# Expert routing in a macaron transformer layer: table products in two halves, expert numbers compared by pairs, ranks summed by halves

## The reference

```python
scores = softmax(xf @ gate_w.T)
_, idx = top_k(scores + gate_b, K)                 # 6 experts for each token
weights = take_along_axis(scores, idx, axis=1)
order = argsort(idx.reshape(-1))                   # by expert, then by token
pos = arange(T * K) - starts[se]                   # rank of a token in its expert
xb = zeros((E, CAP, D)).at[se, pos].set(xf[tok], mode='drop')
h = silu(einsum(xb, w1)) * einsum(xb, w3); yb = einsum(h, w2)
y = scatter-add of yb * weights, for pos < CAP
z = silu(xf @ ws1.T) * (xf @ ws3.T) @ ws2.T        # the shared expert
return y + z
```

## Time and profile before

| | us |
|---|---|
| three runs | 1953.21, 1954.05, 1954.29 |
| median | 1954.05 |
| profiled execution, its device time | 1956.1 |
| profiled execution, first to last instruction (span) | 1954.0 |
| granted TensorE clock, mean share of full speed | 0.974 |

### The profile page before, as it was taken

One profiled execution on the slowest core, in us unless ns is written; L12 is line 12 of the kernel. 1 busy time (PEld: TensorE's weight loads), 2 busy tenths in 40 slices (PEclk: granted clock), 3 DMA queues, 4 the chain that ended last, 5 costly groups with the idle time before them and its releaser, 6 DMA issues. The chain is left out here.

```text
span 1954.0 us, 31890 instructions
## 1 busy us (share of the span) xinstructions
PE 1788.5 (92%) x10553; PEld 1098.4 (56%) x10554; DVE 1337.6 (68%) x3338; ACT 1095.2 (56%) x2260; POOL 836.5 (43%) x923
## 2 busy tenths in 40 slices
PE   6999998999955789999999999999799999989998
PEld 3666665777732344444455454445455656567776
DVE  4878787566537567777777777778268787866664
ACT  4767675111114567777777777776566767631111
POOL 1111110677646565555555555551000101027777
PEclk9999999999978899999999999999999999999999
DMA  2324341899943233333333333332213243339997
GB/s 81 120 86 135 96 125 63 247 258 252 246 74 86 78 85 104 99 95 105 100 98 99 104 102 95 107 91 68 66 49 106 93 139 93 106 97 265 262 265 157
DMA packets 192653, 244.05 MB, mean 125 GB/s; under 512 B 17578, under 2 KB 159978, under 8 KB 192494
## 3 DMA queue, kind: packets, MB, share of 16 engines
q1 hardware_dynamic: 166654, 202.97, 34.6%
q0 software_dynamic: 24576, 37.77, 10.1%
q10 hardware_dynamic: 1264, 1.31, 0.2%
HBM read 126.63 MB, written 63.86 MB: 97 GB/s over the span
## 5 line engine op out<-in xcount | busy, mean ns | idle before, releaser
L1352 DVE TENSOR_REDUCE a_smax<-a_p_ring 128x1 f32<-128x512 f32 (+2 forms) x768 | 353.7, 505 | 151.7 <-PE a_p_ring L1439 146.9
L1257 ACT ACTIVATE a_probs<-a_p_ring 128x512 f32<-128x512 f32 x640 | 364.1, 607 | 103.3 <-PE a_p_ring L1451 102.1
L1439 PE MATMUL a_p_ring<-p_ks,p_qs 100*128 100x512 bf16 (+3 forms) x1024 | 244.9, 304 | 43.2 <-ACT a_probs L1257 20.0
L48 POOL TENSOR_TENSOR f_rstd<-f_mv,eps 128x4 f32<-128x4 f32 x32 | 26.2, 818 | 539.0 <-DVE f_mv L42 534.5
L1451 PE MATMUL a_p_ring<-p_qs,p_ks 103*128 103x512 bf16 (+3 forms) x1024 | 243.7, 305 | 6.0 <-ACT a_probs L1257 5.3
L648 ACT ACTIVATE e_silu<-e_p_up 128x176 f32<-128x176 f32 x128 | 40.6, 317 | 352.8 <-PE e_p_up L738 352.8
L487 PE MATMUL f_p_up<-f_xnT,ws1T 128*128 128x512 f32 x384 | 186.8, 609 | 1.1 <-ACT f_xnT L280 1.1
L528 PE MATMUL f_p_z<-ws2T,f_hidden 128*128 128x256 f32 (+1 forms) x768 | 183.9, 390 | 1.9 <-DVE f_hidden L374 1.9
L127 POOL DMA_INDIRECT h_got<-rows,slot_token x128 | 126.0, 984 | 135.1 <-DVE slot_token L464 86.1
L1467 PE MATMUL a_p_out<-a_probs,p_v 128*32 128x512 f32 (+3 forms) x2048 | 176.6, 445 | 6.5 <-ACT a_probs L1257 6.5
L487 PE MATMUL f_p_up<-f_xnT,ws3T 128*128 128x512 f32 x384 | 180.6, 593 | 0.0
(11 more groups left out here) (156 smaller groups left out, 3573.7 us busy)
## 6 DMA issues: line engine op xcount, KB each, us to landing
h_w<-w_in SPq DMA_DIRECT2D x128, 352.0 KB
p_qs<-a_parts SPq DMA_DIRECT2D x192, 128.0 KB, 2.4
p_ks<-a_parts SPq DMA_DIRECT2D x192, 128.0 KB, 2.5
h_w<-w_in SPq DMA_DIRECT2D x128, 176.0 KB
rows<-f_row SPq DMA_DIRECT2D x32, 640.0 KB, 6.4
x<-x_in SPq DMA_DIRECT2D x16, 512.0 KB, 5.9
acc<-x SPq DMA_DIRECT2D x16, 512.0 KB, 3.3
a_x<-acc SPq DMA_DIRECT2D x16, 512.0 KB, 4.0
```

What stands on the lines that cost most here:

```text
L1257: nc.scalar.activation(to[:], p_score[s][:], ACT.Exp, scale=SCALE).then_inc(score_free[s], 1)
L1352: ins = nc.vector.tensor_reduce(smax[:, t, 4 * g + h:4 * g + h + 1], p_score[s][:, at:at + length], AX.X, ALU.max)
L1439: ins = nc.tensor.matmul(p_score[s][:, at:at + length], qs[1 - u][0:SR + MASK, 4 * g + h, t * P:(t + 1) * P], ks[1 - u][0:SR + MASK, 4 * g ...
```

## The change

Four edits, all in route_and_share.

1. The 24 table products of `add_to_table` are cut into two groups of 12. In a chunk with both neighbours the order on TensorE was turn, 24 products, turn; it is now 12 products, turn, 12 products, turn. The first 12 (tiles 0 and 1) wait for the first at_slot instruction only, the others for the second. In the last chunk both groups of 12 follow one another in both places.
2. topf holds each expert number twice, and pick is compared by pairs of experts, so that no operand has a step of zero in its innermost dimension.
3. The sum over 64 experts is done as two additions of halves (64 to 32, 32 to 16) and a reduction over 16.
4. The final table is read straight from PSUM: the copy is gone, three operations remain.

```diff
-                    nc.vector.tensor_copy(topf[:], topi[:, :, 0:K])
+                    nc.vector.tensor_copy(topf[:], topi[:, :, 0:K].unsqueeze(3).to_broadcast([P, NT, K, 2]))
...
-                    nc.vector.tensor_tensor(pick[:].rearrange("p t k e -> p (t k) e"),
-                                            expert_no[:].unsqueeze(1).to_broadcast([P, NT * K, E]),
-                                            topf[:].rearrange("p t k -> p (t k)").unsqueeze(2).to_broadcast([P, NT * K, E]),
+                    by_twos = [P, NT * K, E // 2, 2]
+                    nc.vector.tensor_tensor(pick[:].rearrange("p t k (e n) -> p (t k) e n", n=2),
+                                            expert_no[:].rearrange("p (e n) -> p e n", n=2).unsqueeze(1).to_broadcast(by_twos),
+                                            topf[:].rearrange("p t k n -> p (t k) n").unsqueeze(2).to_broadcast(by_twos),
                                             ALU.is_equal)
...
+                    by_pair = prod[:].rearrange("p t k e -> p (t k) e")
+                    nc.vector.tensor_tensor(half_sum[:], by_pair[:, :, 0:E // 2], by_pair[:, :, E // 2:E], ALU.add)
+                    dve.drain()
+                    nc.vector.tensor_tensor(half_sum[:, :, 0:E // 4], half_sum[:, :, 0:E // 4],
+                                            half_sum[:, :, E // 4:E // 2], ALU.add)
+                    dve.drain()
...
-                        nc.vector.tensor_reduce(rank[:], prod[:], AX.X, ALU.add)
+                        nc.vector.tensor_reduce(rank[:].rearrange("p t k -> p (t k)"), half_sum[:, :, 0:E // 4],
+                                                AX.X, ALU.add)
...
-                nc.vector.tensor_copy(table[:].rearrange("p a e -> p (a e)"), p_table[:, 0:2 * E])
+                nc.vector.tensor_scalar(empty[:], p_table[:, E:2 * E], 0.0, w.dummy_row[:, 0:1], ALU.is_equal, ALU.mult)
                 dve.drain()
-                nc.vector.tensor_scalar(empty[:], table[:, 1, :], 0.0, w.dummy_row[:, 0:1], ALU.is_equal, ALU.mult)
-                nc.vector.scalar_tensor_tensor(table[:, 0, :], table[:, 1, :], float(P), table[:, 0, :],
-                                               ALU.mult, ALU.add)
+                nc.vector.scalar_tensor_tensor(table[:], p_table[:, E:2 * E], float(P), empty[:], ALU.mult, ALU.add)
                 dve.drain()
-                nc.vector.scalar_tensor_tensor(w.slot_token[:], table[:, 0, :], float(-P), empty[:],
+                nc.vector.scalar_tensor_tensor(w.slot_token[:], p_table[:, 0:E], float(-P), table[:],
...
-                def add_to_table(c):
-                    pe.wait_ge(slots_ready, 2 * c + 2)
+                def add_to_table(c, r):
+                    pe.wait_ge(slots_ready, 2 * c + r + 1)
                     pe.wait_ge(who_ready, c + 1)
-                    for t in range(NT):
+                    for t in (2 * r, 2 * r + 1):
...
-                    ins.then_inc(table_added, 1)
+                    if r == 1:
+                        ins.then_inc(table_added, 1)
...
-                    if left:
-                        turn(c + 1, 0)
-                    if c:
-                        add_to_table(c - 1)
-                    if left:
-                        turn(c + 1, 1)
+                    for r in range(2):
+                        if c:
+                            add_to_table(c - 1, r)
+                        if left:
+                            turn(c + 1, r)
...
                     else:
-                        add_to_table(c)
+                        add_to_table(c, 0)
+                        add_to_table(c, 1)
```

More of the change, by code:

```diff
@@ L171, in route_and_share @@
         expert_no = sb("expert_no", [P, E], BF16)
-        topf = sb("topf", [P, NT, K], BF16)
+        topf = sb("topf", [P, NT, K, 2], BF16)
         pick = sb("pick", [P, NT, K, E], BF16)
@@ L179, in route_and_share @@
         prod = sb("prod", [P, NT, K, E], BF16)
+        half_sum = sb("half_sum", [P, NT * K, E // 2], BF16)
         rank = sb("rank", [P, NT, K], BF16)
@@ L185, in route_and_share @@
         hidden = [sb(f"hidden{j}", [P, T]) for j in range(3)]
-        table = sb("table", [P, 2, E])
+        table = sb("table", [P, E])
         empty = sb("empty", [P, E])
```

## The result

The changed kernel takes 1940.9 us, the median of five executions (1934.3 to 1943.0), beside 1954.3 for five of the kernel before, measured next to them (1953.2 to 1958.0). The medians differ by 13.4 us. The ratio is 0.9913, with a 95% interval of 0.9895 to 0.9932: faster by 0.7 to 1.05%. The forecast was 1939.1 and the range 1934 to 1945.

A forecast was written before the change was run, and what follows sets the result against it. PE was taken to bound the routing stages, busy 284 of 294 us in each. Middle chunks 11.5, pick 1.4 and drain 2.1 sum to 15.0 us, taking the median 1954.05 to 1939.1, range 1934 to 1945.

The forecast's parts named there:

- What bounds: Routing stages: PE works 284 of 294 us and is the bound; only its work or 10 us idle counts mid-stage.
- Middle chunks: Table products in halves bring the second transposes 0.41 us earlier in 28 middle chunks: 11.5 us (9.8 to 14.0).
- Rivals C and D: C: halves give half, 0.1 us per kind change or wait, 1945, chance 0.08. D: middle chunks give nothing, 1950.5, 0.04.
- Pick: Pick by pairs falls from 1758 to 955 ns, counting only in chunk 0: 1.4 us over two layers (0 to 1.7).
- The Trainium skill's rule that I set against it: Full port rate needs runs of two neighbouring 4-byte words; pick would take about 1.47 us and the total be 1939.9.
- The clock in chunk 0: Layer two's chunk 0 runs at granted clock 0.50, rising when it does now; pick's gain there taken as 0.6 us.
- rival B: Less idle keeps the clock up in chunk 0 of both layers: 4.4 us more, 1934.7 to 1937; chance 0.09.
- Ranks and the drain: Last chunk: rank takes 1.62 us for 1753 ns, products start on the first at_slot; drain gives 2.1 us in two layers.
- the table read: Last chunk: slot_token's 1.10 us in four instructions becomes three, 0.2 us less (0 to 0.3).
- a new wait for f_xnT: PE's waits after the change: 0.2 to 0.3 us for f_xnT in 28 places, a sign to look for.
- VectorE was to idle more before f_negmax: Sign after the change: DVE idles more before f_negmax, and longer at the load of x; no size given.
- rival E: DVE's wait for the load of x outgrows 1.16 us of cover and stalls PE in 16 chunks: 1958 and up; chance 0.03.

The follow-up runs named there:

- ranks_between: Changed kernel with the ranks matmuls ahead of the second transposes in all chunks but the first; 1934.5 us, ratio 0.9889 of the kernel before.
- all_first: Changed kernel with all 24 table products ahead of the first transposes and none between the two; 1955.5 us, ratio 0.9998 of the kernel before.
- no_halves: Changed kernel with the 24 table products whole again between the two turns, other edits kept; 1956.2 us, ratio 0.9994 of the kernel before.
- after_b: Second profile of the changed kernel, nothing altered; 1940.3 us.
- no_halves_b: Second profile of the changed kernel with the 24 table products whole again between the two turns; 1956.9 us.
- x_load_first: Changed kernel with each load of x issued ahead of the expert weights' loads; 1943.7 us in one execution.
- pick_only: Kernel before with only topf doubled and pick by pairs; 1952.1 us in one execution.

## Why the prediction was right

**What bounds.** Right. PE sets the period before, after, and in ranks_between, and all further steps moved with it. The idle time in the earlier trace rows was the right row to start from. The products take the same time wherever they stand, so what a chunk loses is idle time of PE: the hole of 0.71 us ahead of the first transposes was filled, and a smaller one opened ahead of the second, where the copy out of p_turn became the limit. 0.39 us went with the halves and another 0.31 with the ranks, 0.70 together, nearly the whole hole.

**Middle chunks.** 0.41 us a chunk was forecast, 11.5 in all, and 0.39 and 10.9 came. Both limits were read rightly from rows: f_row's time after the up group (2.43 forecast, 2.44) and ACT's floor (1.42, 1.42). The missing 0.02 us are of the size of the change from transposes to ranks (0.47 for 0.44). all_first confirms the two limits from the other side, its 0.57 for 0.63 a little low since the floor was 1.38 there. Rivals C and D fall with it: the additional changes between f32 and bf16 and the additional waits cost the period at most 0.02 us and not 0.1.

**Pick.** 955 ns forecast, 958 measured, and 0.78 us in chunk 0 for the 0.80. The Trainium skill's rule that I set against it, Vector Engine (DVE) Microarchitecture Reference, section 5.2, with 1.47 us as the estimate, is not borne out: two bf16 numbers read again and again (958 ns) run at the rate of the longer rows here (955 ns for at_slot and for f_prod). The rule was measured on streams that hop to another word each time, and this one stays.

**The clock in chunk 0.** This is the term that was mis-sized. The forecast held 0.6 us in layer two by the assumption that the clock falls and rises at the same moments, and left the rest to rival B, at a chance of 0.09 for both layers. The profile after shows B: full clock in chunk 0 of both layers, 5.9 us less there in place of 1.4. But it isn't a new state of the kernel. Over all profiles the fall comes in part of the executions: 4 of 4 with the old pick, 7 of 18 with the new one. Summed over those profiles, that is 2.4 us a layer with the old pick and 0.9 with the new, so 3 us in two layers beside the 1.6 of pick itself, an estimate from few profiles. The 4 of 4 are two executions only, so it isn't shown that the edit makes the fall rarer. What the forecast missed is that an event like this comes in some executions and not in others. It was chance, then, that the one profile after showed none, and that of before two. One reading of the prediction was wrong as well: it counts four waits of PE before the fall in layer two. The third ended at 1432.04 and the fourth, 0.27 us, at 1433.23, and the granted clock was 0.50 already from 1432.0.

**Ranks and the drain.** 1.62 us forecast for the rank, 1.61 measured. 1.04 us forecast for the drain, 1.05 and 0.98 measured; 0.67 of it by the halves alone and 0.38 and 0.30 by rank and table in no_halves. Of the 0.2 us forecast for the table read 0.17 came (1.10 to 0.93).

**The sum.** 10.9 + 1.6 + 2.0 = 14.5 us follow from the edits at full clock, against 15.0 forecast. By the medians the gain is 13.4 us at first and 14.6 when measured again; by the ratios it is 17.0 (13.3 to 20.5) and 12.5 (9.6 to 15.3). 14.5 is inside both intervals. With some 3 us of clock it should be over 17, which is inside the first and not inside the second. no_halves speaks against those 3 us too: 1.6 of pick, 0.7 of the drain and 3 would be 5.3, and its interval ends at 4.5. So the timings leave open whether the clock in chunk 0 gives anything in the long run. That the median came within 1.8 us of the forecast proves little by itself, with executions 8 us apart; the terms read in the traces carry the account.

**What was to be seen.** I had named a new wait for f_xnT of 0.2 to 0.3 us in 28 places. The list of waits after has none: the last products overlap the floor in the view, and only 0.10 us lie between their modelled end (1515.14) and the transposes. That PE still idled there was shown by ranks_between, not by a wait. VectorE was to idle more before f_negmax, and did not: 31.8 us in 13 waits before, 33.4 in 14 after, in layer one. Its free time went into the waits for f_capped (1.8 to 2.9 us) and for x (1.6 to 5.8). The cover against rival E held: 5.8 us of VectorE's waits for x in layer one, up to 1.6 at once, and no PE wait. Behind that longest one the add to x ended at 78.31 and f_p_z started at 79.01, so 0.70 us of cover were left where 1.16 had been counted for a middle chunk.

## What to carry to other kernels

When an engine's queue holds a step that waits for nothing near (here products for the chunk before), cut it and put each piece into a hole that another engine's latency makes. Measure each hole by its two limits first, since a piece larger than the hole gives the gain back: all products first cost 16 us, 12 and 12 gained 11. Then ask what still idles behind it; moving ranks by four lines gave another 0.31 us a chunk. For edits off the bound, count the places where the pipeline fills and drains; only there did three of the four edits count, 1.1 us a layer in all at full clock, which the traces show and the times don't.

## What the runs showed of the hardware

The granted clock of TensorE fell to half in chunk 0 in some executions of a kernel and not in others. PE had waited 0.85 and 0.77 us, for f_row and for the copy of f_xnT, before after_b's fall, and as long at the same places in the profile of the same kernel without a fall. In no_halves_b, x_load_first, pick_only and all_first, too, the ranks' matmuls right behind these two waits already ran at half clock in layer one, some 0.05 us apart and not 0.03. The stretch costs 1.1 to 3.2 us. 34 or 35 products of zeros, 1.9 us of mostly idle time, left 0.18 us of the first wait and nothing of the second, and none of the six chunks profiled with such filling had a fall, where 11 of 22 without it had. Why one execution falls and the next doesn't stays open, and the clock fell in some of the drains as well, filled or not. The second surprise is the size of the spread in the stages that no edit touched, 8 us between the profiles of all kernels, of which the runs here do not tell how much is clock.
